# A two-layer decoder on one Trainium2 core: gated experts ranked behind the next chunk's attention, less slack around the last quarter of a recurrence, two bounds on open value sums, and fewer long runs of matmuls

## The reference, cut to what matters

```
x = x + L0_attn (layernorm(x))            # causal self attention, 16 heads of 16
x = x + L0_xattn(layernorm(x), ctx)       # cross attention to 77 context tokens
x = x + L0_ffn  (layernorm(x))            # 8 linear experts, the best 2 weighted
x = x + L1_attn (layernorm(x))            # a recurrence: h = tanh(xt + h @ Wh.T + b), 1024 steps
x = x + L1_xattn(layernorm(x), ctx)       # cross attention again, with biases
x = x + L1_ffn  (layernorm(x))            # a shared gated expert and 16 routed ones, the best 4
```

## Time and profile before

| | us |
|---|---|
| median of the three runs | 1532.84 |
| the profiled execution | 1542.55 |
| its span, first to last instruction | 1540.8 |

### The profile page before, as it was taken

How to read it: one execution, slowest core, us unless ns; L and a number is a source line. 1 busy time by engine, 2 the same in 40 slices (tenths; PEclk the granted TensorE clock), 3 DMA queues, 4 the chain that set the end, 5 groups by cost and what they waited for, 6 DMA issues and landing times.

```text
span 1540.8 us, 48664 instructions
## 1 busy us (share of the span) xinstructions
PE 1492.7 (97%) x20001; PEld 1046.0 (68%) x20001; DVE 804.9 (52%) x2574; ACT 591.4 (38%) x2778; POOL 38.3 (2%) x60
## 2 busy tenths in 40 slices
PE   5699989999999999999999999999999999999998
PEld 4465467777777777777777777777676667665555
DVE  5736753277744217977551126855344534553264
ACT  2051305724313773342268764621243224321220
POOL 1000000000000000000000000000000000000000
PEclk9899889999899999999999999999998999999999
DMA  5644000110000002110000005100001000000100
GB/s 153 136 91 101 22 1 3 24 37 3 2 1 3 3 6 37 30 27 2 2 4 3 3 3 160 30 9 2 1 17 37 2 2 16 3 2 28 22 1 14
DMA packets 45470, 40.20 MB, mean 26 GB/s; under 512 B 9723, under 2 KB 44486, under 8 KB 45254
## 3 DMA queue, kind: packets, MB, share of 16 engines
q1 hardware_dynamic: 43526, 36.32, 10.0%
q10 hardware_dynamic: 1728, 0.79, 0.4%
HBM read 25.81 MB, written 10.80 MB: 24 GB/s over the span
## 4 chain that ended last, share of the span: by engine, by line
PE 92%; DVE 3%; DMA 2%; SPq 1%; issue 0%; ACT 0%; DVEq 0%; ACTq 0%
PE b L512 20%; PE b L531 10%; PE b L1591 8%; PE b L1371 8%; PE b L1643 6%; PE b L1000 5%; PE b L971 4%; PE b L737 4%; PE b L916 3%; PE b L693 3%; DVE mx L925 2%; PE b L1252 2%; PE b L1227 2%; PE b L648 2%; PE b L455 1%; PE b L497 1%
## 5 line engine op out<-in xcount | busy, mean ns | idle before, releaser
L512 PEld LDWEIGHTS b<-hp,whp 128*128 128x128 f16 x12276 | 487.3, 96 | 255.8 <-ACT hp L557 139.5
L512 PE MATMUL b<-hp,whp 128*128 128x2 f16 x12276 | 539.4, 166 | 1.7 <-DVE hp L563 0.6
L563 DVE TENSOR_TENSOR hp<-hist,hp 128x4 f16<-128x4 f32 x1023 | 165.1, 161 | 470.3 <-ACT hist L558 462.4
L557 ACT ACTIVATE hp<-b 128x4 f16<-128x4 f32 x1024 | 177.2, 173 | 538.8 <-PE b L512 530.2
L531 PE MATMUL b<-whp 128*128 128x512 f16 (+5 forms) x829 | 205.3, 352 | 0.0
L925 DVE TENSOR_REDUCE mx<-b 128x1 f32<-128x512 f32 (+3 forms) x304 | 189.0, 653 | 1.7 <-PE b L916 1.2
L558 ACT ACTIVATE hist<-b 128x4 f32<-128x4 f32 x1024 | 178.6, 174 | 0.0
L985 ACT ACTIVATE vp<-b 128x512 f32<-128x512 f32 x288 | 171.3, 602 | 18.7 <-PE b L974 11.1
L1591 PE MATMUL b<-vp,heads 128*128 128x512 f16 x576 | 160.7, 382 | 0.0
L1371 PE MATMUL b<-we,xT 128*128 128x256 f32 x512 | 150.3, 410 | 0.0
L916 PE MATMUL b<-heads 128*128 128x512 f16 (+3 forms) x384 | 115.7, 342 | 3.5 <-DVE mx L925 0.4
(11 more groups left out here) (203 smaller groups left out, 1568.5 us busy)
## 6 DMA issues: line engine op xcount, KB each, us to landing
x_qs<-qx_scr SPq DMA_DIRECT2D x48, 128.0 KB
qx_scr<-xq_pair SPq DMA_DIRECT2D x16, 256.0 KB, 2.1
heads<-q_scr SPq DMA_DIRECT2D x24, 128.0 KB, 4.5
heads<-k_scr SPq DMA_DIRECT2D x36, 64.0 KB, 2.7
x<-in_x SPq DMA_DIRECT2D x8, 256.0 KB, 6.8
q_scr<-tail SPq DMA_DIRECT2D x8, 256.0 KB, 2.3
k_scr<-tail SPq DMA_DIRECT2D x8, 256.0 KB, 2.5
we<-in_L_ffn_We SPq DMA_DIRECT2D x2, 1024.0 KB
```

What stands on the lines that cost most here:

```text
L512: return pe.matmul(self.z(t)[:, m], self.w.whp[:, a, k, m * P:(m + 1) * P], self.g.hp16[:, (t - 1) % 2, part, k, :], start=False, stop=Tru ...
L557: act.activation(self.g.hp16[:, t % 2, 0], self.z(t), ACT.Tanh, scale=1 / LIFT).then_inc(self.s["hi_ready"], 1)
L563: v.tensor_tensor(self.g.hp16[:, t % 2, 1], self.g.hist[:, :, :, t % (4 * HALF)], self.g.hp16[:, t % 2, 0], ALU.subtract).then_inc(self.s[ ...
```

## The change

Five edits, all of them to what the planner is given. No instruction of the model is added or removed; `idle` matmuls and the order can change.

1. `HURRY`, `HURRIED`: once 768 `tanh` operations are placed, the slack is 0.06 us rather than 0.3 us, on every engine.
2. `BEHIND` = 1200: norm and gated experts of chunk c get the ranks 1000 c + 4740 and 1000 c + 4750, which is behind the cross attention of the next chunk (1000 c + 4530).
3. The norm's transposes (`n6_turn`) are placed only after the tile before has been split (`gat_xl`).
4. Values of a group of heads are placed only after `turn_o` of the group two before it, so that at most two such sums are open; in self attention and in cross attention.
5. `BURST_STEPS` = 128 rather than 32.

```diff
--- before.py
+++ after.py
@@ -162,11 +162,14 @@
 SEEN = {"pe": 0.18, "act": 0.10, "v": 0.06, "pool": 0.15, "sp": 2.0}
 PERIOD = 0.79
 LATE = 0.3
+HURRY = 768
+HURRIED = 0.06
 SECOND = 3500
+BEHIND = 1200
 PATIENCE = 6.0
 FULL_CLOCK = 2300
 LEAST_GAP = 0.1
-BURST_STEPS = 32
+BURST_STEPS = 128
 BURST = 1.7
 
 
@@ -244,7 +247,8 @@
                         continue
                     cost = k.cost(k.next)
                     if due is not None and not k.chain and at < due + 0.4:
-                        slack = max(self.late + max(0.0, at - k.ready - PATIENCE) * 0.1, more)
+                        late = self.late if by_name["tanh"].next < HURRY else HURRIED
+                        slack = max(late + max(0.0, at - k.ready - PATIENCE) * 0.1, more)
                         if at + cost > due + slack:
                             continue
                     key = (at, 0 if k.chain and not burst(k) else 1, k.rank(k.next))
@@ -844,7 +848,7 @@
                closes=lambda i: ("self_s", i))
         st.add("pe", "self_values", self.values, len(self.blocks), 0.7, lambda n: of_block(n) + 0.32,
                opens=lambda n: ("self", self.blocks[n][0] // B) if self.blocks[n][0] % B == 0 and self.blocks[n][1] == 0
-               else None)
+               else None, behind=[("self_turn_o", lambda n: self.blocks[n][0] // B - 1)])
         self.merge = Merge(st, "self", [(c, w) for c in range(NK)],
                            lambda u: (self.s["pv"], self.block_end[B * u + 1]), rank, room.merge)
 
@@ -1053,7 +1057,8 @@
         st.add("act", name + "_exp", self.exp, 2 * len(self.units), 0.52, lambda i: of_unit(i // 2) + 0.31,
                closes=lambda i: (name + "s", i))
         st.add("pe", name + "_values", self.values, len(self.units), 0.7, lambda u: of_unit(u) + 0.32,
-               opens=lambda u: (name, u // B) if u % B == 0 else None)
+               opens=lambda u: (name, u // B) if u % B == 0 else None,
+               behind=[(name + "_turn_o", lambda u: u // B - 1)])
         self.merge = Merge(st, name, [(c, w) for c, w, _ in chunks], lambda u: (s["pv"], B * (u + 1)), rank, room.merge)
 
     def zero(self, v, layer):
@@ -1792,11 +1797,11 @@
         rnn = Recurrence(st, rw, ln3, xT3, -5000)
         history = AddHistory(st, rnn, tile_rank(1, 0))
         rnn.back, history_in["rnn"] = history.s["turned"], history.s["xup"]
-        ln6 = ChunkNorm(st, "n6", crossed(1), tile_rank(1, 40), sb("n6_xn", [P, 1, D]),
-                        behind=[("gat_make", lambda i: 12 * MH * (i // TC))])
+        ln6 = ChunkNorm(st, "n6", crossed(1), tile_rank(1, 40 + BEHIND), sb("n6_xn", [P, 1, D]),
+                        behind=[("gat_make", lambda i: 12 * MH * (i // TC)), ("gat_xl", lambda i: i - 1)])
 
         gated_room.room_in = (attn.merge.s["y"], 2 * NH)
-        gated = GatedExperts(st, w, ln6, rank(1, 50), out, gated_room)
+        gated = GatedExperts(st, w, ln6, rank(1, 50 + BEHIND), out, gated_room)
 
         def load(sp, i):
             if i == 0:
```

## The result

The changed kernel takes 1483.91 us, the median of four runs (1469.44 to 1485.18), against 1532.68 us before (four runs). The ratio is 0.9662, with a 95% interval of 0.9611 to 0.9713. The prediction was 1489 us in a range of 1455 to 1525.

What follows compares the result with a forecast made beforehand. Bounds: the pace of the last 256 steps, work left behind them, and cross 3's 70 us, 45 of them empty. 1540.8 - 32 (edits 1 and 2) - 12 (long runs) = 1497 us of span, 1489 us median, range 1455 to 1525.

Steps and rivals of the forecast that it cites:

- The account of work: Behind step 768 TensorE has 67 us of steps and 298 us of other work to do, in whatever order.
- The time of a step: Last 256 steps: 0.86 us each with 0.45 us of other work, instead of 1.13 us; recurrence ends 69 us sooner.
- predicted tail: Behind the last step: 298 - 115 = 183 us of other work remain after the recurrence ends at 1317 us.
- The empty 45 us of cross 3: Behind the recurrence: gated 1 and gated 2 fill the empty time of cross 3, with 8 us lost, between 0 and 20.
- The long runs: Before step 768: 18 of 24 long runs go, 21 us, of which 12 us reach the end, between 0 and 21.
- The halt: Recurrence waiting for layer 0's experts before step 744: a sign of being right was its ending 8 to 15 us sooner.
- Edit 4: Values behind turns: banks come free but values may wait; taken as nothing, between 3 us gained and 5 us lost.
- The clock: Whole span: long runs don't hold the clock, nothing put into the sum; rival that it falls, 1555 us median, chance 0.06.
- The filler starves: Last 256 steps: slack of 0.06 us bars long operations, gated experts wait; 1511 to 1542 us; chance 0.12 in part, 0.08 in full.
- The rank does nothing: Cross 3: gated 2 still finished early, the 45 us stay, only long runs gain; 1521 us, chance 0.09 including cancelling gains and losses.
- More is gained: Cross 1 and cross 2: gated experts fill their idle matmuls too, up to 15 us beyond the lower bound, 1440 us; chance 0.05.

Runs made afterwards that it cites:

- no_patience: Changed kernel, but behind step 768 the slack stays 0.06 us however long an operation has been ready; 1546.38 us, ratio 1.0078.
- long_patience: Changed kernel, but behind step 768 slack grows with waiting only for operations of more than 0.48 us; 1486.01 us, ratio 0.9681.
- no_idle: Changed kernel's order with the idle matmuls left out; 1554.79 us, ratio 1.0160 to the kernel before.
- no_runs: Changed kernel without any long run (BURST_STEPS 4096 instead of 128); 1469.10 us, ratio 0.9587 to the kernel before.
- u_hurry: Changed kernel with edit 1 undone, the slack 0.3 us for all steps; 1506.07 us, ratio 0.9818 to the kernel before.
- u_runs: Changed kernel with edit 5 undone, a long run in front of one step in 32; 1499.44 us, ratio 0.9775.
- combined: Changed kernel without long runs, slack 0.12 us from step 740, growing only for operations of more than 0.48 us; 1469.16 us, ratio 0.9585.
- u_rank: Changed kernel with the ranks of edit 2 undone (BEHIND = 0); 1501.78 us, ratio 0.9793 to the kernel before.

## Why the prediction was right, point by point

**The account of work, right.** 298 us of other work and 67 us of steps behind step 768 is what the changed kernel and all others show, within 8 us once half clock is taken off. So is the place of the larger gain: idle matmuls behind 768 went from 369 to 151, 47 us. Of the 73 us between the profiles, 46 lie behind step 768 (41 at equal clock), for which the prediction had 32, and 27 before it (17 at equal clock), for which it had 12.

**The time of a step, wrong.** 0.86 us with 0.45 us of other work was said; 1.02 us with 0.68 us was measured ((261 - 67 - 96 x 0.214) / 256). Its bound, 0.90 us, was missed too. The step that failed is "with 0.06 us none fits between `hi` and `lo`": it left out the slack's growth, which the same part names for the starving rival and not for products. Under the new ranks gated experts wait, and what waits gets slack. no_patience and long_patience have the 0.83 and 0.90 us when the growth is gone. The recurrence so ended at 1331 us, not at 1305, and 125 us of other work were left behind it (137 less 55 idle matmuls), not 183.

**Why the sum came out all the same.** By the account, a product placed in a step is one less behind it. The predicted tail was long by what the predicted steps were short, 58 us of other work, and the two errors cancel by the way the sum is built. Only the idle matmuls count. The sum had 256 x (0.86 - 0.26 - 0.45) = 38 us of them among the steps and 8 behind, 46 us in all, and the profile has 21 and 12, 33 us. The size of that term was 13 us too pessimistic.

**The empty 45 us of cross 3, right.** 8 us were to be lost of them, between 0 and 20; 55 x 0.214 = 12 us were. That edit 1 and edit 2 belong together was right: each alone leaves 116 and 118 idle matmuls behind the last step, with both there are 55. It wasn't seen that each does a good part of it by itself.

**The long runs, in the range.** 12 us, between 0 and 21: 5 us alone (4 at equal clock), 15.5 us when undone (12). The reason for a discount was right, the halt; its size was not the same in both orders. The halt was to end 8 to 15 us sooner and ended 21 us sooner by the profiles, of which some 10 us are clock. The share "where TensorE is what layer 0 waits for" can't be read off busy times alone.

**Edit 4, right in size, wrong in importance.** Nothing, between 3 us gained and 5 lost, was said; 7 us gained were measured, with 2 to 10 by the interval and 2.5 at equal clock. But the edit is what makes an order possible at all with the other edits. The prediction looked at what values wait for, and not at who gets the banks.

**The clock, right in not counting on long runs.** no_idle has 0.862 to 0.880 once the idle matmuls are gone, and no_runs 0.975 to 0.981 without any long run. The Trainium skill ("TensorE: Matmul & The Clock Gate", "Why this matters for your kernels") has sustained matmul work as what gives the full clock. no_idle agrees with that; that the long runs carry it, as the prediction let the rule say, is refuted by no_runs. Nothing was put into the sum for the clock. Five executions of the changed kernel have 0.973 in the middle, 37 of the kernel before 0.978, which is about 5 us of the medians; whether the change does that, so few executions don't show.

**The rivals.** *The filler starves* didn't happen in the change but did in no_patience, by its own formula: other work there is 211 - 67 - 373 x 0.214 = 64 us among 256 steps, 0.25 us a step; at 0.25 us the formula has 1537 us, and the span was 1539.1 us. That closeness is luck: step 768 came 17 us sooner than the formula has it, and behind the steps 27 us were idle, not 8. The growth of the slack is what keeps the change on the right side of it. *The rank does nothing*: it alone brings 26 us. *More is gained*: the steps in which cross 1 and cross 2 stand did take in gated experts (163 idle matmuls to 96, 14 us), which was held to be the unlikely extra.

**The chances.** They leave more outside of the range than the 0.18 of the text: slower 0.14 and the same 0.05 are 0.19 by themselves, and a part of *More is gained* lies below 1455 us.

**The median.** 49 us gained for 44 predicted. At equal clock it is 54 us, so the sum was 10 us short (13 by the idle matmuls), and the lower clock of the changed kernel's runs brought the measured median nearer to it. The forecast was good for its account of the work; that it came within 5 us was in part luck.

## What to carry to other kernels

Where a list of work is packed around a chain on one engine, count the engine's empty time from a point to the end, wherever it stands. The pace of the chain is worth nothing by itself; slack moves work from one side of its end to the other, which pays where that work then stands in a wait. Read a scheduler's tolerance with all its terms, for the queue that the change itself makes: a term for long waits undid a part of what the constant said, and without it the same constant made the kernel slower than before. Compare kernels that are a few per cent apart with their clocks beside them, and don't take single edits' gains as parts of a sum. And hold work back on purpose for the latencies of the last stage, but look first at who will hold the buffers then.

## What the runs showed of the hardware

The granted clock differs from run to run of one and the same program, and the time with it. 21 runs of the kernel before range from 1529.20 us at 0.983 to 1541.59 us at 0.972: 12.4 us for 2 x 0.011 x 1535 = 34 us more at half clock, 0.37 us for each. A straight line through all 21 gives 0.34, and the changed kernel's five 0.36, so the second digit is open. The two profiles of before and after differ by 42 us at half, 16 of their 73 us, so that profiles of kernels that differ by a per cent have to be compared with their clocks beside them.

With the idle matmuls of up to 512 columns the clock of the changed kernel is 0.973 to 0.987, and the same order without them has 0.862 to 0.880. Single long runs in front of a step have no such effect that these runs could show: with 31 of them the kernels have 0.968 to 0.986, with 7 of them 0.973 to 0.987 (the changed kernel), with none 0.975 to 0.981 (no_runs).

Behind step 768, five profiles have 24 to 41 us at half clock (u_hurry, u_runs, long_patience, no_runs, combined), no_patience 5, the changed kernel and u_rank none. Their steps take 1.17, 1.11, 0.90, 1.02 and 0.90 us, and 0.83, 1.02 and 0.96 us, so it isn't the pace of the steps that decides. What does is open.
